# A kernel of attention and top-1 experts whose block of engine programs closes without GpSimd's own drain

## The chip, the cores and the metric

The kernel runs on one core of one Trainium2 chip. The core has five engines, each with an instruction stream of its own: TensorE (PE, with its weight loads as PEld), VectorE (DVE), ScalarE (ACT), GpSimd (POOL) and SyncE (SP). They meet only by semaphores. The metric is the device time of one execution in microseconds.

## The reference

One transformer layer over an input of 8 x 512 tokens of width 128. First a layer norm, attention with 16 heads of width 8 in a causal window of 32 tokens, a projection, and the residual; then a second layer norm, a router over 8 choices of which 7 are experts, and the output of a shared feed-forward network plus the chosen expert's:

```python
x = x + _L0_attn_ref(_layernorm(x), W_qkv, b_qkv, W_out, b_out)
...
probs = softmax(x @ w_router)                  # 8 choices; index 7 has no expert
topk_vals, topk_idx = jax.lax.top_k(probs, 2)
...
for i in range(TOPK - 1):                      # only the first choice is used
    ...
    out = out + ALPHA * topk_vals[..., i:i + 1] * gathered
shared = x @ ws_up * silu(x @ ws_gate) @ ws_down
return out + shared
```

## The kernel before

The kernel writes each engine's program out by hand and wraps the five of them in one block: the lines `@block.sync`, `@block.gpsimd`, `@block.scalar`, `@block.vector` and `@block.tensor` each hand over one engine's program, and all order between engines comes from some hundred named semaphores. The first half of the time is attention, in 16 pairs of token tiles, then comes the shared network, then the experts.

For the experts the tokens are sorted. GpSimd scatters each of the 32 tiles of 128 tokens with indirect DMAs into `sorted_rows` in HBM (24 whole ones on line 621, 16 halves on line 628). The sorted rows make 38 tiles of 128 rows with one expert each. In step `s` TensorE computes tile `s`, VectorE multiplies by the gate and adds the base into `y` (line 1246, semaphore `y_ready`), and GpSimd's function `write` (line 653) scatters the 128 rows of `y` to their places in the output, again with an indirect DMA. `y` is a ring of four buffers; the landing of a scatter is counted on `written[r]`.

The end of GpSimd's program, which matters here, is this:

```python
            for i in range(MT):
                write(i, i % RING)
            for r in range(RING):
                pool.wait_ge(written[r], 16 * ((MT - 1 - r) // RING + 1))
```

So GpSimd waits on line 662 until every output scatter has landed; nothing in the kernel follows. Behind the five programs the block itself appends a closing part, whose instructions all carry line 69 (the `with ctx:` that the block is left by). In the kernel before it has one drain per engine. That of SyncE, ScalarE, VectorE and TensorE also raises a semaphore `gather` by one. GpSimd first drains, then waits until `gather` is 4, then raises `release`, for which the four others wait. The program's start, line 1644 in the trace, has the same five drains and the same meeting.

The two lines of the kernel that the change and the closing part hang on are 269, where the block is opened, and 69.

Of the kernel before, what the change touches and what calls it, by code (L numbers as in the profile page):

```python
# [8 lines left out]
def windowed_attention_top1_moe_kernel(  # L9
# [58 lines left out]
    ctx = ExitStack()  # L68
    with ctx:
# [196 lines left out]

        x_rows = x.rearrange("b (k p) d -> p (b k) d", p=P)

        block = ctx.enter_context(nc.Block())

        after = {}

# [1381 lines left out]
```

## Time and profile before

| | |
|---|---|
| device time, median of 3 runs | 339.1 us (338.04 to 339.61) |
| span of the profiled execution, first to last instruction | 334.6 us |
| median less that span | 4.5 us |
| PE busy in the span | 306.9 us (92%) |
| POOL busy in the span | 188.4 us (56%) |

Of the profiled execution the trace gives the span alone; the time around it is taken as the difference to the median, 4.5 us. Busy time leaves out instructions that only an engine's sequencer runs: waits on semaphores, branches and drains. Those stand in the rows of a line of the kernel, where an engine's name has a q behind it (POOLq is GpSimd's sequencer).

### The profile page before, as it was taken

To read this page: it belongs to the slowest core of one execution; us is meant where nothing else is said; L and a number is where in the kernel's file an instruction comes from. 1 tells how busy PE (TensorE), PEld (TensorE's weight loads), DVE (VectorE), ACT (ScalarE), POOL (GpSimd) and SP (SyncE) were. 2 spreads that over 40 slices of the span, in tenths; PEclk is the share of its full clock that TensorE was granted. 3 is DMA by queue.
4 is the path that set the end of the run, shared out by engine and by line. 5 is a ranking of instruction groups with operands and counts; after the bars stand their busy time and mean duration, and the time that the engine had idled before them with its cause. 6 is when DMAs were issued, how large, how long until landed. Compare 5 with 4: busy or idle time off the path is not lost. (4 is left out here: it accounts for less than half of the span.)

```text
span 334.6 us, 12234 instructions
## 1 busy us (share of the span) xinstructions
PE 306.9 (92%) x4894; PEld 245.6 (73%) x4894; DVE 216.7 (65%) x456; ACT 151.2 (45%) x268; POOL 188.4 (56%) x290
## 2 busy tenths in 40 slices
PE   8887999999999989997899999999999999999960
PEld 8655757566575756775788888788888888888850
DVE  6797999888979978849863334555555555555520
ACT  3354555444455754821722222335555555555520
POOL 7899567755659638695177775443333333333340
PEclk9999999999999999997999999999999999999996
DMA  7963151322324220796012232233433334333200
GB/s 196 344 161 86 55 121 48 104 63 77 82 69 117 56 62 2 295 360 184 0 50 97 99 113 98 52 78 73 83 71 74 69 70 73 71 72 77 69 9 0
DMA packets 53529, 32.49 MB, mean 97 GB/s; under 512 B 26448, under 2 KB 47700, under 8 KB 53474
## 3 DMA queue, kind: packets, MB, share of 16 engines
q1 hardware_dynamic: 48992, 23.18, 28.4%
q0 software_dynamic: 2880, 6.43, 5.6%
q10 hardware_dynamic: 1602, 2.10, 2.0%
q8 instruction: 40, 0.66, 0.8%
q14 instruction: 15, 0.12, 0.1%
HBM read 13.72 MB, written 11.95 MB: 77 GB/s over the span
## 5 line engine op out<-in xcount | busy, mean ns | idle before, releaser
L653 POOL DMA_INDIRECT out<-y,xn_base x38 | 37.3, 982 | 66.3 <-DVE y L1246 66.3
L1235 DVE TENSOR_TENSOR Pr<-psS,PT 128x512 f32<-128x512 f32 x38 | 26.3, 692 | 30.1 <-PE psS L1581 29.4
L737 ACT ACTIVATE Pr<-psS 128x1024 f32<-128x1024 f32 x32 | 32.8, 1025 | 21.4 <-PE psS L1332 21.4
L1595 PE MATMUL psB<-down_sb,Pr 128*128 x304 | 40.3, 276 | 1.4 <-ACT Pr L866 0.8
L1051 DVE TENSOR_TENSOR hT<-psS,PT 128x512 f32<-128x512 f32 x32 | 22.0, 689 | 28.9 <-PE psO L1485 21.5
L820 ACT ACTIVATE PT<-psS 128x512 f32<-128x512 f32 x32 | 19.1, 597 | 47.2 <-PE psS L1458 36.8
L900 DVE TENSOR_REDUCE row_max<-psS 128x16 fp32r<-128x1024 f32 x32 | 37.6, 1216 | 3.7 <-PE psS L1320 3.7
L1595 PEld LDWEIGHTS psB<-down_sb,Pr 128*128 128x128 f32 x304 | 36.9, 192 | 1.7 <-issue 1.7
L955 DVE STREAM_TRANSPOSE PT<-Pr 128x1024 f32<-128x1024 f32 x32 | 37.4, 1205 | 0.2 <-ACT Pr L737 0.2
L863 ACT ACTIVATE PT<-psS 128x512 f32<-128x512 f32 x38 | 22.7, 597 | 27.1 <-PE psS L1575 27.1
L866 ACT COPY Pr<-psO 128x512 f32<-128x512 f32 x38 | 22.3, 587 | 21.4 <-PE psO L1587 21.4
L621 POOL DMA_INDIRECT sorted_rows<-rows,pos_u x24 | 23.0, 960 | 8.0 <-issue 7.0
L628 POOL DMA_INDIRECT sorted_rows<-rows,half_pos_u x16 | 16.0, 997 | 20.3 <-DVE rows L1098 10.8
L1485 PEld LDWEIGHTS psO<-down_sb,hT 128*128 128x128 f32 x224 | 26.1, 192 | 1.4 <-issue 0.8
L1485 PE MATMUL psO<-down_sb,hT 128*128 128x128 f32 x224 | 26.4, 276 | 0.0
L1320 PE MATMUL psS<-Kx,Qx 32*32 32x256 f32 x1024 | 25.7, 381 | 0.0
L1246 DVE SCALAR_TENSOR_TENSOR y<-psB,xn_base 128x128 f32<-128x128 f32 x38 | 13.4, 351 | 18.9 <-PE psB L1595 18.2
L484 POOL TENSOR_TENSOR rows<-rows,proj 128x256 f32<-128x256 f32 x15 | 10.9, 730 | 25.9 <-ACT proj L743 25.7
L1332 PE MATMUL psS<-row_max,minus_ident 128*128 128x512 f32 x64 | 22.4, 431 | 0.4 <-DVE row_max L900 0.4
L1587 PE MATMUL psO<-ident,Pr 128*128 128x128 f32 x152 | 22.7, 272 | 0.0
L1587 PEld LDWEIGHTS psO<-ident,Pr 128*128 128x128 f32 x152 | 18.8, 139 | 4.8
L1320 PEld LDWEIGHTS psS<-Kx,Qx 32*32 32x32 f32 x1024 | 17.7, 103 | 2.9 <-issue 0.5
(202 smaller groups left out, 684.2 us busy)
## 6 DMA issues: line engine op xcount, KB each, us to landing
sorted_rows<-pad_rows SPq DMA_DIRECT2D x9, 528.0 KB, 5.3
xn_base<-sorted_rows SPq DMA_DIRECT2D x38, 66.0 KB, 2.0
xs<-sorted_rows SPq DMA_DIRECT2D x152, 16.0 KB
rows<-in_L_attn_x SPq DMA_DIRECT2D x8, 256.0 KB, 6.0
VD_even<-V SPq DMA_DIRECT2D x28, 72.0 KB, 2.6
VD_odd<-V SPq DMA_DIRECT2D x28, 72.0 KB, 2.4
gate_sb<-in_L_ffn_w_gate ACTq DMA_DIRECT2D x1, 1792.0 KB, 12.2
Kx<-K SPq DMA_DIRECT2D x28, 64.0 KB, 2.4
```

The costliest lines, as they stand in the source:

```text
L621: pool.indirect_dma_start(out=sorted_rows, out_offset=bass.IndirectOffsetOnAxis(pos_u[:, g : g + 1], 0), in_=rows[:, g, :, :].rearrange("p ...
L653: pool.indirect_dma_start(out=out_list, out_offset=bass.IndirectOffsetOnAxis(tok_u[:, r, :], 0), in_=y[:, r, :], in_offset=None, bounds_ch ...
L737: nc.scalar.activation(Pr[:, half, :], psS[:, half, :], ACT.Exp, scale=SCALE).then_inc(exp_done, 1)
L863: nc.scalar.activation(sg[:, r % 2, :], psS[:, r % 2, 512:], ACT.Silu).then_inc(esilu_done, 1)
L900: nc.vector.tensor_reduce(row_max[:, half, :], s, AX.X, ALU.max).then_inc(max_done, 1)
L955: nc.vector.transpose(PT[:, half, :], Pr[:, half, :]).then_inc(pt_done, 1)
L1235: nc.vector.tensor_tensor(hs[:, r % 2, :], psS[:, r % 2, 0:512], sg[:, r % 2, :], ALU.mult).then_inc(eh_done, 1)
L1320: last = mm(psG[j * BLK : (j + 1) * BLK, g, t * HPG * KEYS : (t + 1) * HPG * KEYS], Qx[r, b % 2, at : at + BLK], Kx[r, b % 2, :, at : at + ...
L1332: last = mm(psG[:, half * GPH + n, :], minus_ident[:, :], m.unsqueeze(2).to_broadcast([P, HPB, KEYS]), start=False, stop=True, skip_group_ ...
L1485: last = mm(psO[:, 1, k * D : (k + 1) * D], hT[:, c, k * P : (k + 1) * P], down_sb[:, SHARED, c * D : (c + 1) * D], start=(c == 0), stop=( ...
L1587: last = nc.tensor.transpose(psO[:, r % 2, hidden], hs[:, r % 2, hidden], ident[:, :])
L1595: last = mm(psB[:, 0:D], hsT[:, r % 2, c * P : (c + 1) * P], down_flat[:, bass.ds(start + c * D, D)], start=(c == 0), stop=(c == NC - 1),)
```

## The change

The block is opened with an argument more. The instructions of the five programs, their order and their waits stay as they are.

```diff
-        block = ctx.enter_context(nc.Block())
+        block = ctx.enter_context(nc.Block(no_gpsimd_drain=True))
```

What it does to the closing part, as the built program has it (`gather` and `release` are the block's own two semaphores; PL is GpSimd; the four lines of ACT stand for PE, DVE and SP as well):

```diff
-ACT Drain           wait release==0   gather++1
+ACT Drain
+ACT EventSemaphore  wait release==0   gather++1
 ACT EventSemaphore  wait release>=1   release--1
...
-PL  Drain
 PL  EventSemaphore  wait gather>=4    gather-=4
 PL  EventSemaphore                    release+=4
```

GpSimd's drain is gone, and the four other engines raise `gather` in an instruction of its own behind their drain. The start of the program keeps all its five drains.

## Rows read from the trace of the kernel before

**Rows 1.** The page's first lines: span, then busy us (share) and instructions.

```profile
span 334.6 us, 12234 instructions
PE 306.9 (92%) x4894; PEld 245.6 (73%) x4894; DVE 216.7 (65%) x456; ACT 151.2 (45%) x268; POOL 188.4 (56%) x290
```

**Rows 2.** The page's 40 slices of the span, busy tenths of PE and POOL.

```profile
PE   8887999999999989997899999999999999999960
...
POOL 7899567755659638695177775443333333333340
```

**Rows 3.** Timeline, last rows: start us, us, engine, line, [idle before].

```profile
323.24 0.98 POOL L653 DMA_INDIRECT out<-y,xn_base  x1 [0.77 <-DVE y L1246]
323.73 0.97 PEld L1595 LDWEIGHTS psB<-down_sb,Pr 128*128 128x128 f32 x8 [0.96 <-issue]
323.76 1.13 PE L1595 MATMUL psB<-down_sb,Pr 128*128 x8 [0.75 <-ACT Pr L866]
324.93 0.35 DVE L1246 SCALAR_TENSOR_TENSOR y<-psB,xn_base 128x128 f32<-128x128 f32 x1 [1.97 <-PE psB L1595]
325.56 0.98 POOL L653 DMA_INDIRECT out<-y,xn_base  x1 [1.34 <-DVE y L1246]
```

**Rows 4.** Line 662, GpSimd's last waits: ns min/median/max, first and last start.

```profile
L662 POOLq EVENT_SEMAPHORE  x2: 17/1156/2294, 325.3 to 325.4; - x2
```

**Rows 5.** Line 69, the block's closing part on the five sequencers.

```profile
L69 POOLq EVENT_SEMAPHORE  x2: 17/17/17, 334.4 to 334.5; - x2
L69 SPq DRAIN  x1: 128/128/128, 318.7 to 318.7; - x1
L69 ACTq DRAIN  x1: 614/614/614, 323.1 to 323.1; - x1
L69 PEldq DRAIN  x1: 783/783/783, 324.2 to 324.2; - x1
L69 DVEq DRAIN  x1: 391/391/391, 324.9 to 324.9; - x1
L69 POOLq COMPARE_BRANCH  x1: 41/41/41, 327.7 to 327.7; - x1
L69 POOLq DRAIN  x1: 6447/6447/6447, 327.9 to 327.9; - x1
L69 SPq EVENT_SEMAPHORE  x1: 17/17/17, 334.5 to 334.5; - x1
...
L69 PEldq EVENT_SEMAPHORE  x1: 51/51/51, 334.5 to 334.5; - x1
```

**Rows 6.** Busy time by stretch: us, the five engines, PEclk, DMA, GB/s.

```profile
326.60:327.90 1.30, 0.00 (x0) 0.00 (x0) 0.00 (x0) 0.00 (x0) 0.00 (x0) 1.00 0.02 0
327.90:334.60 6.70, 0.00 (x0) 0.00 (x0) 0.00 (x0) 0.00 (x0) 0.00 (x0) 0.56 0.00 0
```

**Rows 7.** Line 1644, the program's start, its drains and a constant's memset.

```profile
L1644 SPq DRAIN  x1: 7/7/7, 0.0 to 0.0; - x1
L1644 DVEq DRAIN  x1: 10/10/10, 0.1 to 0.1; - x1
...
L1644 POOLq DRAIN  x1: 173/173/173, 0.4 to 0.4; - x1
L1644 POOL MEMSET const-uint8-127<- x1: 101/101/101, 0.4 to 0.4; 128x1 uint8 x1
```

**Rows 8.** Lines 653 and 621: GpSimd's indirect DMAs, then time to landing.

```profile
L653 POOL DMA_INDIRECT out<-y,xn_base x38: 982/982/994, 226.9 to 325.6; - x38
...
DMA to landing us min/median/max: 2.1/2.4/3.9
L621 POOL DMA_INDIRECT sorted_rows<-rows,pos_u x24: 954/960/963, 177.0 to 206.8; - x24
...
DMA to landing us min/median/max: 2.4/2.4/3.2
```

**Rows 9.** Page part 5, the 16 half scatters of line 628.

```profile
L628 POOL DMA_INDIRECT sorted_rows<-rows,half_pos_u x16 | 16.0, 997 | 20.3 <-DVE rows L1098 10.8
```

## The prediction

> **What bounds the kernel now.** I read the page first. TensorE is busy for 306.9 us of a span of 334.6 [rows 1], and its row of slices stays at 7 to 9 tenths until the 38th slice, then falls to 6 and 0 [rows 2]. So TensorE is the bound nearly everywhere, and the change touches no instruction of that part; all that it can touch is the last slice and a half. One slice is 334.6 / 40 = 8.4 us, so the digit 0 is a whole slice in which nothing computes.
>
> The timeline of the last microseconds says what ends the work: the last matmuls start at 323.76, VectorE's last `y` runs from 324.93 to 325.28, and GpSimd issues the last output scatter at 325.56 for 0.98 us [rows 3]. After 326.6 no engine is busy for the 8.0 us that are left, and in the last 6.7 of them the DMA engines move nothing either [rows 6]. The rows of single lines fill the gap. GpSimd's wait on line 662 lasts 2294 ns from 325.4, to 327.7: that is the landing of the last scatter [rows 4]. Then follow a branch at 327.7 and, at 327.9, GpSimd's drain of 6447 ns. It ends at 327.9 + 6.4 = 334.3, GpSimd's two semaphore instructions follow at 334.4 and 334.5, and the four others pass at 334.5; the last of these takes 51 ns, and that is the end of the span at 334.6 [rows 5]. The reader is to see that the drain is 6.4 of the last 6.7 us, that all four other engines have waited for it since 325.3 at the latest (VectorE's drain is the last, 324.9 + 0.391), and that all data had landed before it began.
>
> **The change part by part.** What is removed is one instruction, GpSimd's drain of 6.447 us [rows 5]. Its semaphore instruction, now at 334.4, would follow the branch instead, at the drain's old start of 327.9. Nothing else has to be waited for there: the four `gather` increments are due from drains that start at 318.7, 323.1, 324.2 and 324.9, and end by 325.3 [rows 5]. Removing it therefore takes 6.447 us and the few hundredths between its end (334.34) and the next instruction (334.4) off the chain: 6.5 us.
>
> What is added are four semaphore instructions, one on each other engine. Such an instruction takes 17 ns on SyncE and 51 ns on TensorE [rows 5]. They lie under GpSimd's wait on line 662, which ends 327.7 - 325.3 = 2.4 us after the last of their drains; I cost them at nothing. Without that cover VectorE's would be on the path, between 0.02 and 0.05 us.
>
> Next in line once the drain is gone is the landing of the last scatter. Landings take 2.1 to 3.9 us, 2.4 in the median [rows 8]; this one took 325.56 to 327.7, about 2.1, and the wait is the same wait with the same releaser as before. It could come later in another execution, by at most 3.9 - 2.1 = 1.8 us, in either kernel.
>
> The sum: span 334.6 - 6.5 = **328.1 us**. The trace gives no time of the profiled execution beyond its span; the median of the runs, 339.1, stands 4.5 us above it, and with 4.5 us unchanged around the span the time is 328.1 + 4.5 = **332.6 us**, 1.9% less. The spread of the runs shown, 338.04 to 339.61, is 0.46% of 339.1, so 0.5% (1.7 us) is about what can be told from no change.
>
> **What the drain may be made of.** This is the disputed point, since nothing in the trace shows what the 6.447 us are spent on. The nearest rows lie far apart. The other drain of the same engine, at the start, takes 173 ns, and that is the rest of its memsets: the last begins at 0.4 as the drain does and runs 101 ns [rows 7]. By that row an idle GpSimd drains in under 0.2 us. Between the two drains lie 38 + 24 + 16 = 78 indirect DMAs [rows 8, 9], so I take it that the long drain belongs to them: either a fixed step, or work that the engine still has with them, 6447 / 78 = 83 ns each. A growing backlog would show as later landings, but the median landing is 2.4 us for the first group as for the last [rows 8], so I lean to a step that the drain itself starts and that is gone with it. The bounds are: all of 6.5 us saved, and none of it.
>
> The Trainium skill bears on this in "PSUM — Partial Sum Buffer", section "Engine vs sequencer instructions": a drain waits until its engine is fully idle. No engine instruction of GpSimd runs after 326.6 here [rows 6], so by that rule read plainly the drain should be as short as the start's, and the sum would be 0.2 us, to 338.9; the measured 6.447 us says that something unseen is drained, and it is the row that I sum with.
>
> **The rivals.** *Moved behind the program.* The 6.447 us are work of GpSimd that is due in any case, and whoever needs the engine idle next pays for it: what runs in the 4.5 us around the span, which no row shows, or the drain at the next start, now 173 ns [rows 7]. The span of the profile would then fall to 328.1, and the time around it rise from 4.5 to 11.0; or the start's drain would grow to some 6.4 us and the span stay. The time is 339.1, no change. For it speaks that no row explains what the drain does; against it the landings that show no backlog, and that 4.5 us of surroundings hold no second step of 6.4 us in the kernel before. The Trainium skill has a sentence that favours it: "VectorE: DVE Perf Modes", section "The DRAIN you can't avoid", says that the launch's own preamble and postamble put short drains on all five engines. No trace here shows them; by that rule with a backlog the time would be 339.1.
>
> *Partly moved.* The same work goes on beside whatever closes the execution outside the span. If all 4.5 us around the span lay behind the program and ran beside it, 6.5 - 4.5 = 2.0 us would be left to wait for: 332.6 + 2.0 = 334.6 us.
>
> *Paid twice, slower.* If the work is started by every drain that follows indirect DMAs rather than done once, then without the drain in the program both a drain outside the span and the one at the next start (173 ns now [rows 7]) could meet an engine that was not put in order, at 6.4 us each: 332.6 + 2 x 6.4 = 345.4 us. It takes 6.5 + 1.7 = 8.2 us of such cost, 1.3 drains' worth, before the kernel is slower by more than 0.5%. Nothing in the rows speaks for it; against it, the start's drain shows no trace of anything left by an earlier execution, though that one did drain.
>
> *No effect on the program.* Were the drain still there, line 69 would show it and the time would be 339.1. The closing part as it is built has none, so this adds only a little to the case of no change.
>
> **How the numbers follow.** Full gain, 332.6: 0.72. Moved or no effect, 339.1: 0.15. Partly moved, 334.6 or thereabouts: 0.08. Slower: 0.05. The likeliest case alone carries the spread of the runs and a landing that comes a little earlier or later: 331.6 to 333.9. To leave out no more than 2 in 10, the range has to reach over the partial case too; from 331.6 to 336.0 it holds 0.80. Chances: faster 0.80 (the first and third case), same 0.15, slower 0.05.
>
> **What the changed profile would show.** A span of 328.1 and no drain of POOLq on line 69, with POOLq's semaphore instructions at about 327.9. The drains of the four others would start where they do now, at 318.7 to 324.9, each with a semaphore instruction behind it that ends by 325.4; the wait on line 662 still some 2 us, and everything before 325 in its place within the noise. The start's drain on POOLq should stay at 173 ns. A start's drain of microseconds, or a time more than 6 us above the new span, would say that the cost has moved. The prediction is wrong if GpSimd's unseen work is owed in any case.

## The result, and the profile after

The changed kernel takes 332.3 us (median of 4 runs, 331.65 to 333.31), the kernel before 338.6 us in the same comparison (336.72 to 339.61). The ratio is 0.985 with a 95% interval of 0.981 to 0.989. A longer comparison (below, first experiment) gave 331.0 against 337.8 us, ratio 0.981, 0.976 to 0.985. The medians lie 6.2 and 6.8 us apart. Some executions of either kernel are slower and show a lower granted clock; the medians, ratios and intervals of this document leave out those that took over 1.5% more than the fastest of their kernel. The drain of 6.447 us would by itself give 1 - 6.5 / 337.8 = 0.981: the middle of the second interval and the edge of the first.

Line 69 of the changed kernel, the block's closing part (duration ns min/median/max, first and last start us), answers to [rows 5]:

```profile
L69 SPq EVENT_SEMAPHORE  x2: 17/17/17, 320.9 to 329.9; - x2
L69 ACTq EVENT_SEMAPHORE  x2: 17/17/17, 325.6 to 329.9; - x2
L69 PEldq EVENT_SEMAPHORE  x2: 51/51/51, 326.9 to 330.0; - x2
L69 DVEq EVENT_SEMAPHORE  x2: 21/21/21, 327.3 to 330.0; - x2
L69 POOLq EVENT_SEMAPHORE  x2: 17/17/17, 329.8 to 329.9; - x2
...
L69 DVEq DRAIN  x1: 389/389/389, 326.9 to 326.9; - x1
L69 POOLq COMPARE_BRANCH  x1: 41/41/41, 329.6 to 329.6; - x1
```

GpSimd's drain is gone: its semaphore instruction starts at 329.8, 0.2 us behind the branch at 329.6. In [rows 5] the branch at 327.7 was followed by 6.4 us of drain. VectorE's added semaphore instruction, the last of the four, starts at 327.3 and lies under GpSimd's wait on line 662 as the four did in the plan:

```profile
L662 POOLq EVENT_SEMAPHORE  x2: 17/1155/2293, 327.2 to 327.3; - x2
```

If what the drain does were owed at the next start, GpSimd's drain there would grow. It stands on line 1644 of the changed kernel and answers to [rows 7]:

```profile
L1644 POOLq DRAIN  x1: 174/174/174, 0.4 to 0.4; - x1
```

174 ns against 173: nothing is owed at this start. Which kernel ran just before a profiled execution is not on record, but in all twelve traces of this case, eight of them of programs whose block closes without GpSimd's drain, the start's drain takes 172 to 190 ns. The measured time around the span has not grown either. The profiled execution's own time was 331.73 us with a span of 330.0, so 1.7 us lie around it. In the runs of the kernel before that came with the experiments the same 1.7 or 1.8 us lie around the span (337.3 us with a span of 335.6, 336.05 with 334.3).

The two profiled spans, 334.6 and 330.0, differ by 4.6 us and not by 6.5. The changed kernel's last scatter was issued later, so the difference arose before the end. The last two rows of its timeline, against [rows 3]:

```profile
326.85 0.35 DVE L1246 SCALAR_TENSOR_TENSOR y<-psB,xn_base 128x128 f32<-128x128 f32 x1 [1.97 <-PE psB L1595]
327.47 0.98 POOL L653 DMA_INDIRECT out<-y,xn_base  x1 [1.33 <-DVE y L1246]
```

That is 1.9 us later than 324.93 and 325.56. GpSimd's first half scatter (line 628) already starts at 168.6 us and not at 166.3 us, so the delay is there by then. The stretch 160 to 176 us of the two executions (us, busy us and instructions of PE, PEld, DVE, ACT, POOL, then granted clock, DMA share, GB/s) shows one place where they part. The changed kernel:

```profile
160.00:176.00 16.00, 14.59 (x90) 13.07 (x89) 9.68 (x23) 7.17 (x11) 5.85 (x6) 0.90 0.07 22
```

The kernel before:

```profile
160.00:176.00 16.00, 14.60 (x94) 12.77 (x93) 11.61 (x26) 7.43 (x12) 7.54 (x8) 1.00 0.08 26
```

The granted clock is 0.90 on average against 1.00, so for part of the stretch it was at the lower of its two levels (1.2 and 2.4 GHz), and 4 matmuls fewer stand in it. TensorE's busy time, 14.6 us of 16, is the same. In the second execution of the changed kernel that was profiled (below) this stretch has a clock of 1.00, that scatter starts at 166.0, the last one at 325.98, and the span is 328.5. So this is a difference between executions and not between kernels.

### The profile page after: what moved, and what is told of

Read it like the earlier page. It is cut to its first block and busy times, and to the rows that moved or that the text cites. A ratio compares the mean times of both kernels' runs of the same rounds, so it can differ in the third digit from the quotient of the medians.

```text
span 330.0 us, 12237 instructions
## 1 busy us (share of the span) xinstructions
PE 309.0 (94%) x4894; PEld 247.8 (75%) x4894; DVE 216.7 (66%) x456; ACT 151.5 (46%) x268; POOL 188.7 (57%) x290
## 5 line engine op out<-in xcount | busy, mean ns | idle before, releaser
L1485 PEld LDWEIGHTS psO<-down_sb,hT 128*128 128x128 f32 x224 | 27.7, 201 | 1.5 <-issue 0.8
L1485 PE MATMUL psO<-down_sb,hT 128*128 128x128 f32 x224 | 27.8, 284 | 0.0
```

The lines of the kernel that those rows point to most:

```text
L1485: last = mm(psO[:, 1, k * D : (k + 1) * D], hT[:, c, k * P : (k + 1) * P], down_sb[:, SHARED, c * D : (c + 1) * D], start=(c == 0), stop=( ...
```

## The experiments

**The same kernel in more rounds.**

> The changed kernel once more, in more rounds beside the kernel before. If the whole drain is gained, the two medians differ by 6.5 us (ratio 0.981), and the time around the span is the same in both; if part of the drain had moved behind the program, the time around the span would be larger than that of the kernel before by that part.

Measured: 331.0 us (6 runs, 330.24 to 332.51) against 337.8 (16 runs), ratio 0.981 (0.976 to 0.985). The profiled execution took 330.24 us with a span of 328.5: again 1.7 us around it. The gain is whole, and none of it has moved into the measured time around the span.

**The drain written by hand.**

```diff
             for r in range(RING):
                 pool.wait_ge(written[r], 16 * ((MT - 1 - r) // RING + 1))
+            pool.drain()
```

> The changed kernel with one drain written by hand as the last instruction of GpSimd's program. All else of the closing part stays as changed. If the drain alone is the gain, line 69's missing drain comes back here at 6.4 us and the time is that of the kernel before (ratio 1.00). If the gain came from the way in which the other four engines raise their semaphore, the time stays at 0.98.

Measured: 338.8 us against 337.8, ratio 1.002 (0.999 to 1.006), on the changed kernel's closing part. The drain, now on a line of its own, reads

```profile
L663 POOLq DRAIN  x1: 6445/6445/6445, 329.9 to 329.9; - x1
```

So the drain is the whole of the gain, and the four added semaphore instructions cost nothing that can be measured.

**Two drains in a row.**

```diff
+            pool.drain()
+            pool.drain()
```

> The same with two drains in a row. A step of fixed price that each drain starts: 6.4 us each, span longer than the changed kernel's by 12.9. Work that is owed once (a backlog of 83 ns for each of 78 indirect DMAs, or a state to be put in order): 6.4 us and then under 0.2 us.

Measured, the two lines of that kernel:

```profile
L663 POOLq DRAIN  x1: 6445/6445/6445, 329.3 to 329.3; - x1
...
L664 POOLq DRAIN  x1: 34/34/34, 335.8 to 335.8; - x1
```

The second takes 34 ns, and the span is 336.1 us. A fixed price per drain is out; something is owed once. Whether it is a count or a state, this run cannot say.

**What the drain counts.** A kernel of its own, with GpSimd writing constant rows to the output and drains between; its core is

```python
            pool.drain()                       # line 46
            several(0, 1)                      # indirect DMAs, then waits for all to land
            pool.drain()                       # line 48
            pool.drain()                       # line 49
            several(1, 9)
            pool.drain()                       # line 51
            several(9, 10)
            pool.memset(small[:, :], 1.0).then_inc(go, 1)
            pool.wait_ge(back, 10)             # VectorE's ten long memsets
            pool.drain()                       # line 55
            several(10, 11)
            pool.memset(small[:, :], 2.0).then_inc(made, 1)
            pool.wait_ge(made, 3)
            pool.drain()                       # line 59
            several(11, 12, plain)             # one plain DMA of GpSimd
            pool.drain()                       # line 61
            several(12, 32)
            pool.drain()                       # line 63
```

> A small kernel that leaves the whole computation out and only writes constant rows to the output from GpSimd, with eight drains between. Before any DMA; after 1 indirect DMA that has landed; again at once; after 8 indirect DMAs; after 1 indirect DMA and some 20 us of idling; after 1 indirect DMA and a memset; after 1 plain DMA of the same engine; after 20 indirect DMAs. Backlog of 83 ns each: 0.2, 0.2, 0.2, 0.7, 0.2, 0.2, 0.2, 1.7 us. A fixed step of every drain once DMAs have been issued: 0.2 and then 6.4 each time. A state that one drain puts in order: 0.2, 6.4, 0.2, 6.4, and 6.4 for each of the others that follows a DMA.

Measured, by line:

```profile
L46 POOLq DRAIN  x1: 46/46/46, 1.2 to 1.2; - x1
...
L48 POOLq DRAIN  x1: 131/131/131, 4.5 to 4.5; - x1
...
L49 POOLq DRAIN  x1: 34/34/34, 4.6 to 4.6; - x1
...
L51 POOLq DRAIN  x1: 706/706/706, 16.6 to 16.6; - x1
...
L55 POOLq DRAIN  x1: 129/129/129, 45.7 to 45.7; - x1
...
L59 POOLq DRAIN  x1: 113/113/113, 49.0 to 49.0; - x1
...
L61 POOLq DRAIN  x1: 118/118/118, 51.5 to 51.5; - x1
...
L63 POOLq DRAIN  x1: 1682/1682/1682, 78.7 to 78.7; - x1
```

0, 1, 8 and 20 DMAs since the drain before give 46, 131, 706 and 1682 ns. From 1 to 8 that is (706 - 131) / 7 = 82 ns each, from 8 to 20 (1682 - 706) / 12 = 81 ns. A line of 49 + 82 n ns gives 6445 ns for the 78 indirect DMAs of the kernel; 6447 and 6445 were measured. Neither of the other two theories fits: the price is by the count. And the work does not run off by itself: after one DMA and some 25 us of idling the drain still takes 129 ns, as at once. A memset behind the one DMA (line 59, 113 ns) and a plain DMA in place of the indirect one (line 61, 118 ns) change little.

**The second small kernel**, with drains behind other kinds of work:

```python
            several(0, 8, lambda g: rows_of(g, 32))    # indirect, 32 rows each
            pool.drain()                               # line 53
            several(0 + 8, 16, plain)                  # plain DMAs, 128 rows
            pool.drain()                               # line 55
            several(16, 20)
            ...                                        # memset, 20 us of idling
            several(20, 24)
            pool.drain()                               # line 60
            ...                                        # memset, 20 us of idling
            pool.drain()                               # line 63
            scatter(24)                                # not waited for
            pool.drain()                               # line 65
            pool.wait_ge(landed[24], 16)
            several(25, 31)
            ...                                        # a memset
            pool.drain()                               # line 70
            several(31, 32)
            pool.drain()                               # line 72
```

> A second small kernel that leaves the whole computation out. Drains after: 8 indirect DMAs of 32 rows; 8 plain DMAs of GpSimd with 128 rows; 8 indirect DMAs of which 4 have 20 us of idling behind them; nothing but a memset and 20 us of idling; 1 indirect DMA that has not landed; 6 indirect DMAs and a memset; 1 indirect DMA. Priced by the DMA: 0.71, 0.71, 0.71, 0.05, 0.13, 0.54, 0.13 us. Priced by the row or descriptor: the first is some 0.2 us. If idling works the backlog off: the third is 0.4 us. If a drain waits for landing: the fifth is about 1.3 us.

Measured:

```profile
L53 POOLq DRAIN  x1: 728/728/728, 12.2 to 12.2; - x1
...
L55 POOLq DRAIN  x1: 696/696/696, 19.2 to 19.2; - x1
...
L60 POOLq DRAIN  x1: 695/695/695, 58.6 to 58.6; - x1
...
L63 POOLq DRAIN  x1: 46/46/46, 84.9 to 84.9; - x1
...
L65 POOLq DRAIN  x1: 2532/2532/2532, 85.4 to 85.4; - x1
...
L70 POOLq DRAIN  x1: 541/541/541, 97.5 to 97.5; - x1
...
L72 POOLq DRAIN  x1: 119/119/119, 101.0 to 101.0; - x1
```

Eight DMAs cost 728, 696 and 695 ns, whether they move 32 rows or 128, are indirect or plain, or have idled for over 20 us in between. Six and a memset cost 541 ns, one costs 119. So the price goes by the instruction and not by its rows. The drain behind a scatter that had not landed took 2532 ns: a drain of GpSimd also waits until its DMAs have landed. The expected 1.3 us counted from the end of the issue, but the row begins before the scatter's own 0.97 us, so the row is longer. In that trace the scatter starts at 85.65 and the drain ends at 87.93, 2.3 us later; scatters of this kernel land after 2.2 to 2.3 us.

**An engine instruction in place of the drain.**

```diff
+            pool.memset(power[:, :], -0.5)
```

> The changed kernel with a small memset, an engine instruction, as GpSimd's last one in place of a drain. If the engine is really busy with something for 6.4 us after its 78 DMAs, the memset starts 6.4 us late or takes that long, and the span is that of the kernel before. If only a drain starts that work, the memset takes 0.1 us, behind the last landing, and the span is the changed kernel's.

Measured, the memset of that kernel, in the timeline behind the last scatter:

```profile
326.80 0.98 POOL L653 DMA_INDIRECT out<-y,xn_base  x1 [1.33 <-DVE y L1247]
328.98 0.10 POOL L663 MEMSET power<- 128x8 f32 x1 [1.21 <-issue]
```

It runs 0.10 us long as soon as the last wait lets it, and the span is 329.2 us. So GpSimd can run an instruction at once after its 78 DMAs. The 6.4 us are spent only if a drain asks for them.

**Five drains in the kernel.**

```diff
             pool.wait_ge(pos_ready, 1)
+            pool.drain()
...
+            pool.drain()
             last_token = pool.to_reg(NT * P - 1)
...
             for i in range(MT):
+                if i in (MT - 8, MT - 1):
+                    pool.drain()
                 write(i, i % RING)
             for r in range(RING):
                 pool.wait_ge(written[r], 16 * ((MT - 1 - r) // RING + 1))
+            pool.drain()
```

> The changed kernel with five drains on GpSimd: before the first scatter, after the 40 scatters of the sorted rows, before the 31st output scatter, before the last one, and at the end. Priced by the indirect DMAs since the drain before (0, 40, 30, 7, 1): 0.05, 3.3, 2.5, 0.6 and 0.13 us, 6.6 us together. With a fixed price: 0.2 and four times 6.4 us.

Measured:

```profile
L636 POOLq DRAIN  x1: 41/41/41, 167.8 to 167.8; - x1
...
L649 POOLq DRAIN  x1: 5895/5895/5895, 222.9 to 222.9; - x1
...
L663 POOLq DRAIN  x2: 2676/3412/4147, 307.4 to 325.5; - x2
...
L667 POOLq DRAIN  x1: 126/126/126, 331.0 to 331.0; - x1
```

The first and the last, behind DMAs that have landed, fit: 41 ns after none, 126 ns after one. The three in the middle were put directly behind a scatter and miss, with 5.9, 4.1 and 2.7 us for 3.3, 2.5 and 0.6: they hold the issue of the scatters ahead of them too. The first of the three starts at 222.9, and the last half scatter is issued until 225.2, so 3.7 us are left for the expected 3.3. The second starts at 307.4 behind a scatter issued until 308.6 and has 3.0 us left for 2.5. The third ends at 328.2, 2.5 us after the start of its scatter, which landed 2.1 us after its start: there the landing is the longer part. The 0.3 to 0.5 us that the first two take beyond the line stay unexplained. What the last drain owes did fall from 6.4 to 0.13 us.

**The debt paid in small coin.** The kernel before with its closing drain, and 38 drains more.

```diff
+            pool.drain()
             last_token = pool.to_reg(NT * P - 1)
...
             for i in range(MT):
                 write(i, i % RING)
+                if i < MT - 1:
+                    pool.drain()
```

> The kernel before, closing drain and all, with 38 more drains where GpSimd waits anyway: one between the scatters of the sorted rows and the first output scatter, and one behind each output scatter but the last. The small kernel gave 131, 706 and 1682 ns after 1, 8 and 20 indirect DMAs, so 0.05 us and 0.082 us for each. By that the first of them takes 3.3 us, the next ones 0.13 us each, and the closing drain 0.13 us: the time is that of the changed kernel plus 0.1 us (ratio to the kernel before 0.981). If a drain also waits for its scatter to land, it takes some 1.3 us, still within the 1.7 us of idling in each step. If a drain has a fixed price in this kernel, the closing drain stays at 6.4 us and the time at that of the kernel before or above.

Measured: 353.5 us against 337.8, ratio 1.047 (1.043 to 1.052). A clear miss. The new drains and the closing one in that kernel's profile:

```profile
L648 POOLq DRAIN  x1: 5652/5652/5652, 224.6 to 224.6; - x1
...
L663 POOLq DRAIN  x37: 2412/2694/3967, 230.9 to 350.3; - x37
...
L69 POOLq DRAIN  x1: 123/123/123, 355.8 to 355.8; - x1
```

The closing drain is down to 123 ns as it should be. The first, on line 648, was expected at 3.3 us and takes 5.65: it starts at 224.6, the last two half scatters are issued until 226.9, and 3.3 us are left. Each drain in the loop takes 2.7 us in the median with the issue and landing of its scatter. That fills the whole step of the kernel before, 318.77 - 316.05 = 2.72 us from scatter to scatter. In this trace the 38 scatters start between 231.1 and 353.4, on average 3.3 us apart; in the kernel before they start between 226.9 and 325.6 [rows 8], 2.7 us apart. The next scatter now waits for the landing of the last one, and by the order of the program `y`'s ring and, behind it, SyncE's loads wait with it: VectorE's transposes, which waited 0.5 us for `xs` in the kernel before, wait 36.1 us in this one. The row of waits:

```profile
DVE xT L1160 <- DMA xs<-sorted_rows: 36.1, 27, 3.1
```

The profiled execution was a long one (a span of 356.1 us, against 350.7 to 354.2 in the runs that the median is of), so its sums are somewhat large.

**One drain under cover.** Only the first of those 38.

```diff
+            pool.drain()
             last_token = pool.to_reg(NT * P - 1)
```

> The kernel before with one more drain, between its 40 scatters of the sorted rows and its 38 output scatters, where GpSimd idles for 4.0 us; the closing drain stays. Priced by the plain and indirect DMAs since the drain before, the closing drain falls from 6.4 to 0.05 + 38 x 0.082 = 3.2 us, and if the new one costs nothing where it stands the time is 338.1 - 3.3 = 334.8 us, ratio 0.990. With five drains the one at this place ended 1 us too late for the first output scatter; if nothing takes up that delay, the ratio is 0.993. With a price that does not go by the count the closing drain stays at 6.4 us and the ratio at 1.00.

Measured on a chip on which the kernel before took 351.8 us: 349.1 us, ratio 0.992 (0.988 to 0.995). The two drains:

```profile
L648 POOLq DRAIN  x1: 4542/4542/4542, 238.8 to 238.8; - x1
...
L69 POOLq DRAIN  x1: 3160/3160/3160, 346.1 to 346.1; - x1
```

The closing drain has 38 DMAs to answer for: 49 + 38 x 82 = 3165 ns by the line, 3160 measured. The covered one holds the issue of the last half scatter, until 239.9, and then takes 3.4 us for its 40 DMAs. It ended at 243.3, before the first `y` at 244.3, so no output scatter waited for it. The expected 3.3 us of gain are 0.9% of 352; the interval holds it, and by itself it would also hold the expected 0.993 of a late scatter, which the trace rules out.

**The drain without the waits ahead of it.**

```diff
-            for r in range(RING):
-                pool.wait_ge(written[r], 16 * ((MT - 1 - r) // RING + 1))
```

> The kernel before with its closing drain, but without GpSimd's waits on line 662 ahead of it: the drain is reached 2.3 us earlier, while the last scatters are still on their way. If its work on the 77 or so DMAs that have been issued before runs beside the last landing, it ends about 6.45 us after the last scatter is issued and not after it has landed: 1.1 us earlier than in the kernel before, ratio 0.997. If it first waits for the landing, the ratio is 1.00.

Measured: ratio 0.998 (0.995 to 1.001), which does not tell the two expectations apart. The profile does:

```profile
344.19 0.98 POOL L653 DMA_INDIRECT out<-y,xn_base  x1 [1.33 <-DVE y L1244]
```

That is the last scatter in the timeline, and this the closing drain on line 69:

```profile
L69 POOLq DRAIN  x1: 7668/7668/7668, 344.0 to 344.0; - x1
```

The drain ends at 344.0 + 7.7 = 351.6, which is 6.5 us after the scatter's issue ended at 345.2. In the kernel before the drain's end at 334.3 came 7.8 us after 326.5. The last scatter lands 2.1 us after its start at 344.19, so at 346.3, and a drain that began its work only then would have ended at about 352.7. So the work on the DMAs already issued runs beside the last landing, and the end comes 1.3 us sooner; the ratio has too wide an interval to confirm the gain.

## Why the prediction was right

The forecast was 332.6 us; 332.3 and, in the longer comparison, 331.0 were measured. Point by point:

*What bounds the end.* Right. The drain of 6.447 us was alone on the path, and with it gone the last landing is, through the same wait of 2.29 us on line 662.

*The price of the edit, 6.5 us.* Right: with the drain put back by hand the time is that of the kernel before, and it is 6.445 us long.

*The four added instructions at nothing.* Right, by the same experiment, and by their starts at 327.3 and before, under a wait that ends at 329.6.

*The 4.5 us around the span.* Wrong in size: each run of both kernels has 1.7 or 1.8 us around its span. By that the profiled execution of the kernel before took some 336.3 us, which is short; its span set against the median of other executions made the difference. The sum used the same 4.5 us on both sides, so the error cancels and the time is simply the median of 339.1 less 6.5. The forecast span of 328.1 did not come out in the first profile (330.0) and nearly did in the second (328.5). The price of the partly moved rival, 334.6, rested on this figure; it could have hidden 1.7 us at the most, for 332.6 + 6.5 - 1.7 = 337.4 us.

*What the drain is made of.* Half right. I leaned to a step that the drain itself starts, and that held: no engine instruction is held up, and idling does not shorten it. I set it against a price per DMA as if the two excluded each other, and there the argument from the landings failed. They show no backlog because nothing is worked off behind them; the work waits for the drain, at 82 ns per DMA. 6447 / 78 = 83 ns was the right figure for it.

*The rivals.* Moved: ruled out, as far as the measured time reaches, by the start's drain (174 ns) and by the 1.7 us around the span; work that falls outside the device time would show in no run here. Paid twice: ruled out by the same, and by the second drain in a row, which takes 34 ns. Partly moved: the 1.7 us have not grown, and the gain is whole. No effect: line 69 has no drain of GpSimd any more.

The Trainium skill's rule in "PSUM — Partial Sum Buffer", section "Engine vs sequencer instructions", that a drain waits for its engine to be fully idle, is not the whole of it here: an idle GpSimd drains in 46 ns if it has issued no DMA since the last drain, and in 6445 ns after 78 that have landed. The 2532 ns behind a scatter in flight show that for GpSimd idle includes its DMAs' landing.

## What to carry to other kernels

Look at the rows of sequencer instructions behind the last busy one: a stretch in which no engine and no DMA is busy can still be one instruction. If GpSimd has issued n DMAs, the drain at a block's end costs about 0.05 + 0.082 n us once they have landed; where the kernel already waits for every landing by semaphore, as this one does on line 662, the block can close without it, and this kernel gained the whole drain. Whether the drain serves anything else, no run here shows. If a drain has to stay, one more where GpSimd idles long enough takes the count off the last, but never directly behind a scatter in a tight loop, since it waits for the landing as well.

## What the hardware showed that I had not expected

GpSimd's drain has a price for each DMA that GpSimd has issued since its last drain: 34 to 46 ns for 0, 113 to 131 for 1, 541 for 6, 695 to 728 for 8, 1682 for 20, 3160 for 38, 6447 for 78, all landed. It is nearly the same for 32 rows and for 128 (728 and 706 ns for eight), for plain and indirect (696 and 706), at once and after over 20 us of idling (131 and 129 for one). Nor does a memset pay the debt (541 ns for six with one behind them). Left unpaid at the program's end, it costs neither that execution nor the next one anything that these runs can show. What the engine does in some 82 ns per DMA no row shows, and that stays open. So does what a much larger number of undrained DMAs would do; 78 is the most that was tried.
